# Sixteen slot-table scatters on GpSimd: taken out of the attention heads and issued in the first eleven slots of the shared experts

## The chip, the cores and the metric

One core of one Trainium2 chip runs the whole program. The metric is device time in microseconds (us), taken as the median of several runs. Lower is better.

## The reference: what is computed

One transformer layer on x (4 batches, 512 tokens, 512 features) and a context (4, 512, 256). First cross attention, then a mixture of experts:

```
x = x + xattn(layernorm(x), ctx)            # 16 heads of 32, softmax, keys 0..495 and 16 "dca" keys apart
h = layernorm(x)                            # 2048 tokens
scores = softmax(h @ gate_w.T)              # 64 experts
w6, e6 = top_k(scores, 6); w6 /= sum(w6)    # 12288 (token, expert) pairs
pos = place of the pair among its expert's pairs;  dropped if pos >= 384
y[token] += w6 * expert_e(h[token])         # silu(h@wg.T) * (h@wu.T) @ wd.T, 352 wide
out = x + y + shared_expert(h)              # 704 wide, every token
```

## The kernel before, in words

Everything is fp32. Products that need accuracy are split into a rounded high part and a rest (names ending in `_hi`, `_lo`). Each engine has its own written-out program, and semaphores tie them together.

**Heads.** The 2048 tokens are 16 tiles of 128; there are 64 heads (4 batches of 16). A loop over `UNITS`, u = 0 to 15, does four heads each (`n = 4 * u` and on) and threads through them the work of several tiles at different stages: the q, k and v products of later tiles, the output projection of tile u - 5 (`wo_product`), its second layer norm, and the routing of tile u - 6. On TensorE a head is: transposes of the negated maxima (`shift_turned`, L1400), score products (L1415), transposed score products (`turn_scores`, L1425), and the weighting of the values of the head before (`weigh`, L1441 and L1444). VectorE takes the maxima (`maxima`, L643 to L645) and divides (`weighted`, L654, L656), ScalarE takes the exponentials (`exps`, L1104). GpSimd adds the two attention results of each head (`join`, L451), adds a bias (`with_bo`, L479), scales q and k (`scaled`, L442) and adds the mask of a tile to a running count (`counted_on`, L488).

**Routing of one tile j.** TensorE computes its logits (`route_logits`, L1503), VectorE copies them out (`take_logits`, L731) and TensorE's next `shift_turned` into the same bank waits for that copy. VectorE finds the six experts, TensorE the positions (`route_pos`), and VectorE writes, for each of 128 tokens, six slot numbers into `slot` and six pairs of (token number, weight) into `rows`; then `slot_ready` rises. These two buffers hold all 16 tiles, each in a place of its own.

**The scatter.** GpSimd writes the pairs of tile j to `slot_table` in HBM with six indirect DMAs, one for each of the token's experts, 128 rows of 8 bytes each (`scatter(j)`, L462). Each adds 16 to `tab_in`. Tiles 0 to 9 (`GROUP1` is 10) are routed in the heads, tile j in unit j + 6; tiles 10 to 15 are routed together in the first slots of the shared experts.

**Shared experts.** 16 slots, eight token blocks of 256 by two halves of the shared expert. In a slot TensorE does three gate/up chunks (`gate_up`, L2390, 24 matmuls each), then the down product of the item before (`down`, L2408), with transposes of the next block between (`transpose_chunk`, L2373). ScalarE takes the silu of a chunk (L2221), VectorE multiplies (L2297), and so on. TensorE may be up to three chunks ahead of VectorE's product (`sets = 3`). At named points of a slot a callback, `side(slot, point)`, does the rest of the heads' work: the layer norm and routing of the last tiles. On GpSimd only the point "rows" is used, at the head of the slot, and GpSimd has nothing else to do until it copies ids for the first routed expert. SyncE waits at the start of slot 11 for `tab_in` to reach 16 * 6 * 16, then loads the whole table; VectorE reads it in slot 12. After the 16 slots come the 64 routed experts, whose rows are gathered and added back by indirect DMAs.

**GpSimd's order in a unit of the heads** is: `scatter(u - 7)`, `join(n - 1)`, a part of the weights (`wo_part`), `with_bo(u - 2)`, `join(n)`, `counted_on`, `scaled` twice, a bias, `join(n + 1)`, a bias, `join(n + 2)`. After the last unit it does `join(63)`, `with_bo` twice and `scatter(9)`.

Of the kernel before, what the change touches and what calls it, by code (L numbers as in the profile page):

```python
# [58 lines left out]
TILES = NB * T  # L59
# [5 lines left out]
GROUP1 = TILES - 6  # L65
# [42 lines left out]
def attention_phase(nc, ctx, K, ins, hbuf, x1d, table, kvd, qkd):  # L108
    with ExitStack() as here:
# [18 lines left out]
        carry, slot, rows, xc, h2T, bst, mv2, eps5 = K.carry, K.slot, K.rows, K.xc, K.h2T, K.bst, K.mv2, K.eps5  # L128
# [144 lines left out]
        def tile(j):  # L273
            return 0 <= j < TILES
# [4 lines left out]
        def keys_of(j):  # L279

            return P - DCA if j % T == T - 1 else P
# [153 lines left out]
        def heads_gpsimd(pool, net):  # L435
            def scaled(j, v, col, given, done):
                if not tile(j):
                    return
                pool.wait_ge(rs_ready.sem, rs_ready.value(j - 5, 0))
                g = heads_of(v[:, j % 2, :])  # L440
                scale = rs[:, (j - 5) % 2, col:col + H]
                pool.tensor_tensor(g, g, bc(scale.unsqueeze(2), [P, H, HD]), ALU.mult).then_inc(done.sem, 1)  # L442

            def join(n):
                if not head(n):
                    return
                b, h = n // H, n % H
                pool.wait_ge(pv_taken.sem, pv_taken.value(n, 1))
                if h == 0 and b >= 2:
                    pool.wait_ge(aoT_ready.sem, aoT_ready.value((b - 1) * T - 1, 1))  # L450
                pool.tensor_tensor(ao_of(b)[:, :, h * HD:(h + 1) * HD], pv2[:, n % 2, :, 0, :],  # L451
                                   pv2[:, n % 2, :, 1, :], ALU.add).then_inc(head_done.sem, 1)

            def scatter(j):
                if not tile(j):
                    return
                if j == 0:
                    pool.wait_ge(scratch_and_wo, SCRATCH_AND_WO)
                pool.wait_ge(slot_ready.sem, slot_ready.value(j, 1))
                pool.sem_inc(passed, 1)  # L460
                for k in range(TOPK):
                    pool.indirect_dma_start(  # L462
                        out=table, out_offset=bass.IndirectOffsetOnAxis(slot[:, j, k:k + 1], 0),
                        in_=rows[:, j, k, :], in_offset=None, bounds_check=E * CAP - 1,
                        oob_is_err=False).then_inc(tab_in, 16)

            def biased(j, m, v, bias, raw, done):
                if not tile(j):
                    return
                pool.wait_ge(raw.sem, raw.value(j, 1))  # L470
                pool.tensor_tensor(v[0:m, j % 2, :], v[0:m, j % 2, :], bias[0:m, :], ALU.add).then_inc(done.sem, 1)

            def with_bo(j):
                if not tile(j):
                    return
                if j == 0:
                    pool.wait_ge(scratch_and_wo, SCRATCH_AND_WO)
                pool.wait_ge(xc_in[j % 2].sem, xc_in[j % 2].value(j // 2, 16))
                pool.tensor_tensor(xc[:, j % 5, :], xc[:, j % 5, :], bo[:], ALU.add).then_inc(xb_ready.sem, 1)  # L479

            def counted_on(j):
                if not tile(j):
                    return
                pool.wait_ge(mask_ready.sem, mask_ready.value(j, 1))
                if j >= 1:
                    pool.wait_ge(carry_ready.sem, carry_ready.value(j - 1, 1))
                    pool.wait_ge(pos_ready.sem, pos_ready.value(j - 1, 1))
                pool.tensor_tensor(carry[:, (j + 1) % 2, :], carry[:, j % 2, :], mask[:], ALU.add).then_inc(carry_ready.sem, 1)  # L488
# [105 lines left out]
            def wo_part(c):  # L594
                if c == 0:
                    pool.wait_ge(scratch_and_wo, SCRATCH_AND_WO)
                    pool.wait_ge(kvd_ready, 1)
                if c >= DC:
                    return
                src = wo_in_place[:, c * D:(c + 1) * D]  # L600
                pool.tensor_copy(wo_hi[:, c, :], src)
                pool.drain()
                pool.tensor_tensor(wo_lo[:, c, :], src, wo_hi[:, c, :].bitcast(F32), ALU.subtract).then_inc(pool_split, 1)
# [3 lines left out]
                front(u + 7)  # L607
            for u in UNITS:
                n = 4 * u
                scatter(u - 7)  # L610
                join(n - 1)
                wo_part(u)

                with_bo(u - 2)
                join(n)

                counted_on(u - 6)
                scaled(u + 5, kb, H, k_sum, kn_ready)
                scaled(u + 5, qb, 0, q_sum, qn_ready)
                biased(u + 6, P, qb, bq, q_raw, q_bias)  # L620
                join(n + 1)

                biased(u + 6, keys_of(u + 6) if tile(u + 6) else P, kb, bk, k_raw, k_bias)
                join(n + 2)
            join(HEADS - 1)
            with_bo(TILES - 2)
            with_bo(TILES - 1)
            scatter(GROUP1 - 1)

            def side(slot, point):  # L630
                if point == "rows" and GROUP1 <= slot + 4 < TILES:
                    scatter(slot + 4)
            return side

# [752 lines left out]
        def heads_tensor(pe, net):  # L1387
# [396 lines left out]
            def side(slot_no, point):  # L1784
# [21 lines left out]
                elif here == (5, "chunk1"):  # L1806
# [3 lines left out]
            return side  # L1810

        return dict(sync=heads_sync, gpsimd=heads_gpsimd, vector=heads_vector, scalar=heads_scalar, tensor=heads_tensor,
                    over_made=over_made, h2_out=h2_out, x1_out=x1_out, wo_ready=wo_ready)

# [1012 lines left out]
```

## Time and profile before

| | |
|---|---|
| median of 3 runs | 1850.05 us (1841.58, 1850.05, 1877.37) |
| the profiled execution's own time | 1846.09 us |
| its span, first to last instruction | 1844.4 us |
| mean granted TensorE clock | 0.955 of full |
| busy: TensorE matmuls, VectorE, ScalarE, GpSimd | 1766.3, 1091.5, 1029.9, 742.0 us |
| heads | about 88 to 675 us of the span |
| shared experts' slots | about 690 to 897 us |

Times in the text are microseconds from the start of the span. A line such as L1503 is a line of the kernel file. PE is TensorE's matmul row and PEld its weight loads, DVE is VectorE, ACT is ScalarE, POOL is GpSimd, SP is SyncE. PEclk is the granted TensorE clock: 1.00 is 2.4 GHz, 0.50 is 1.2 GHz.

### The profile page before, as it was taken

Reading aid. Unit: us, or ns where it says so; the run is one execution under the profiler, and the core shown is the slowest. Engines: PE = TensorE matmul, PEld = TensorE weight load, DVE = VectorE, ACT = ScalarE, POOL = GpSimd, SP = SyncE. Lnnn points to the kernel's source line nnn. Section 1 sums busy time; section 2 is a strip of 40 time slices with the busy share of each in tenths; the row PEclk is TensorE's granted clock in tenths of the full one; section 3 lists DMA queues with packets and bytes.
Section 4 is the critical chain, followed back from the end, with each engine's and each line's share of the span. In section 5 each row is a group of like instructions: output and inputs, shape, how many; then the busy total and the mean of one; then the engine's idle time right before and its main releaser. Section 6 shows DMA issues by size and latency. Waiting matters only on the chain.

```text
span 1844.4 us, 36478 instructions
## 1 busy us (share of the span) xinstructions
PE 1766.3 (96%) x12110; PEld 1614.3 (88%) x12110; DVE 1091.5 (59%) x2166; ACT 1029.9 (56%) x1879; POOL 742.0 (40%) x711
## 2 busy tenths in 40 slices
PE   3799999999999999999999999999999999999997
PEld 3588888888888878999999999999999999999986
DVE  6555657666555644434466666666666666666655
ACT  4567666556534535112366666666666666666654
POOL 6522222333213220034035555555555545555532
PEclk8999999899769879999999999999999999999988
DMA  5533433332312512411268777777777777786765
GB/s 179 163 109 105 111 98 104 98 88 84 90 58 61 175 40 81 150 65 53 88 199 242 207 217 221 209 229 209 239 202 222 216 214 223 215 232 204 234 185 167
DMA packets 149083, 289.89 MB, mean 157 GB/s; under 512 B 29198, under 2 KB 66318, under 8 KB 139648
## 3 DMA queue, kind: packets, MB, share of 16 engines
q1 hardware_dynamic: 116112, 238.21, 39.6%
q0 software_dynamic: 32880, 50.51, 13.0%
q8 instruction: 52, 0.85, 0.2%
q14 instruction: 39, 0.32, 0.1%
HBM read 243.73 MB, written 64.52 MB: 167 GB/s over the span
## 4 chain that ended last, share of the span: by engine, by line
PE 85%; DVE 4%; issue 4%; ACT 2%; POOL 1%; DVEq 1%; another core or an unknown queue 1%; DMA 1%; SPq 0%; ACTq 0%; POOLq 0%
PE ps L2390 36%; PE ps L2408 18%; PE ps L1444 8%; PE ps L1452 5%; PE ps L1425 4%; PE ps L2373 3%; PE ps L1415 3%; PE ps L1441 2%; PE ps L1467 1%; PE ps L1400 1%; PE ps L2712 1%; PE ps L1461 1%; DVE nmax L643 1%; DVEq L645 0%
## 5 line engine op out<-in xcount | busy, mean ns | idle before, releaser
L2140 POOL DMA_INDIRECT out<-y,ids_s x128 | 204.8, 1600 | 283.5 <-ACT y L2271 258.7
L2390 PE MATMUL ps<-xt_hi,gu_hi 128*128 128x256 f32 (+1 forms) x1920 | 313.6, 285 | 0.0
L2390 PE MATMUL ps<-xt_lo,gu_hi 128*128 128x256 f32 (+1 forms) x1920 | 299.8, 278 | 0.0
L2390 PE MATMUL ps<-xt_hi,gu_lo 128*128 128x256 f32 (+1 forms) x1920 | 299.2, 278 | 0.0
L1104 ACT ACTIVATE prob<-ps 128x512 f32<-128x512 f32 x256 | 151.9, 597 | 238.2 <-PE ps L1425 193.9
L2175 DVE TENSOR_TENSOR gu_lo<-raw_gu,gu_hi 128x1408 fp32r<-128x1408 f32 x132 | 214.5, 1625 | 114.0 <-ACT gu_hi L2172 104.1
L2390 PEld LDWEIGHTS ps<-xt_hi,gu_hi 128*128 128x128 f32 (+1 forms) x1920 | 259.4, 180 | 6.9
L2390 PEld LDWEIGHTS ps<-xt_lo,gu_hi 128*128 128x128 f32 (+1 forms) x1920 | 252.1, 179 | 0.0
L2390 PEld LDWEIGHTS ps<-xt_hi,gu_lo 128*128 128x128 f32 (+1 forms) x1920 | 251.8, 179 | 0.0
L2120 POOL DMA_INDIRECT xg<-h_rows,ids_g x128 | 192.9, 1507 | 119.9 <-POOL ids_g L2115 50.6
L2228 ACT ACTIVATE h_hi<-h 128x256 fp32r<-128x256 f32 (+1 forms) x240 | 100.5, 419 | 227.2 <-DVE h L2297 226.7
L1444 PE MATMUL ps<-v_main,prob 128*128 128x33 f32 x1536 | 225.7, 287 | 0.0
L1444 PEld LDWEIGHTS ps<-v_main,prob 128*128 128x128 f32 x1536 | 212.2, 209 | 0.0
L643 DVE TENSOR_REDUCE nmax<-ps 128x2 fp32r<-128x992 f32 x128 | 152.3, 1189 | 74.7 <-PE ps L1415 68.8
L2221 ACT ACTIVATE sg<-ps 128x256 f32<-128x256 f32 (+1 forms) x240 | 90.9, 379 | 180.8 <-PE ps L2390 128.5
L2172 ACT ACTIVATE gu_hi<-raw_gu 128x1408 fp32r<-128x1408 f32 x132 | 180.8, 1370 | 0.0
L462 POOL DMA_INDIRECT slot_table<-rows,slot x96 | 97.0, 1011 | 163.1 <-DVEq L1061 135.1
L2297 DVE TENSOR_TENSOR h<-sg,ps 128x256 f32<-128x256 f32 (+1 forms) x240 | 99.4, 414 | 76.7 <-ACT sg L2221 63.8
L2408 PE MATMUL ps<-d_hi,h_hi 128*128 128x512 f32 (+1 forms) x480 | 138.1, 396 | 0.0
L2408 PE MATMUL ps<-d_lo,h_hi 128*128 128x512 f32 (+1 forms) x480 | 137.9, 395 | 0.0
L2408 PE MATMUL ps<-d_hi,h_lo 128*128 128x512 f32 (+1 forms) x480 | 137.9, 395 | 0.0
L1425 PE MATMUL ps<-qs,ks 128*128 128x512 f32 x256 | 131.8, 516 | 0.7 <-ACT qs L1096 0.7
(305 smaller groups left out, 3041.0 us busy)
## 6 DMA issues: line engine op xcount, KB each, us to landing
raw_gu<-in_w_gu SPq DMA_DIRECT2D x71, 1408.0 KB
raw_d<-in_w_d SPq DMA_DIRECT2D x71, 512.0 KB
raw_d<-in_w_d SPq DMA_DIRECT2D x71, 192.0 KB
qs<-qk_rows SPq DMA_DIRECT2D x192, 64.0 KB, 1.9
ks<-qk_rows SPq DMA_DIRECT2D x192, 64.0 KB, 2.0
xa<-in_x SPq DMA_DIRECT2D x16, 256.0 KB, 2.9
qk_rows<-k_hi SPq DMA_DIRECT2D x16, 256.0 KB, 2.2
qk_rows<-k_lo SPq DMA_DIRECT2D x16, 256.0 KB, 2.5
```

The source lines that it names most:

```text
L643: dve.tensor_reduce(nmax[:, n % 2, t, 0], ps[:, SCB:SCB + 2, 0:MAIN], AX, ALU.max, negate=True)
L1104: act.activation(prob[:, n % 2, c, :], ps[:, STB + c % 2, :], ACT.Exp).then_inc(prob_ready.sem, 1)
L1425: pe.matmul(ps[:, STB + c % 2, :], ks[:, n % RING, c * P:(c + 1) * P], qs[:, n % RING, :], start=True, stop=True).then_inc(sT_ready.sem, 1)
L1444: last = pe.matmul(ps[:, POB, o:o + HD + 1], prow[:, c, :], v_main[:, b % 2, c, h, :], start=False, stop=c == T - 2)
L2120: pool.indirect_dma_start(out=B.xg[:, p, k, :], out_offset=None, in_=hbuf, in_offset=bass.IndirectOffsetOnAxis(B.ids_g[:, p, k:k + 1], 0), ...
L2140: pool.indirect_dma_start(out=out, out_offset=bass.IndirectOffsetOnAxis(B.ids_s[:, p, k:k + 1], 0), in_=B.y[:, p, k, :], in_offset=None, b ...
L2172: eng.activation(hi, raw, ACT.Copy).then_inc(gu_hi.sem, 1)
L2175: eng.tensor_tensor(B.gu_lo[:, p, half], raw, hi.bitcast(F32), ALU.subtract).then_inc(gu_lo.sem, 1)
L2228: act.activation(B.h_hi[0:m, it.half, c, 0:W], B.h[0:m, (it.half * NF + c) % 2, 0:W], ACT.Copy).then_inc(h_hi.sem, 1)
L2297: dve.tensor_tensor(B.h[0:m, b, 0:W], B.sg[0:m, b, 0:W], gu_banks(c, m)[1], ALU.mult).then_inc(h_ready.sem, 1)
L2390: last = pe.matmul(gu_banks(c, m)[half], w[:, p, half, d, o:o + m], x[:, x_p, d, 0:W], start=i == 0, stop=i == len(steps) - 1)
L2408: last = pe.matmul(ps[:, Y0 + k % 2, :], h[0:m, p, c, k * P:(k + 1) * P], w[0:m, p, c, :], start=begins and i == 0, stop=ends and i == len ...
```

## The change

The scatters of tiles 0 to 9 leave the heads. In the callback, slots 0 to 4 issue two tiles each (0 and 1, 2 and 3, up to 8 and 9), and slots 6 to 11 issue tiles 10 to 15 as before. The number of indirect DMAs stays at 96; nothing else is touched.

```diff
             for u in UNITS:
                 n = 4 * u
-                scatter(u - 7)
                 join(n - 1)
                 wo_part(u)
...
             with_bo(TILES - 2)
             with_bo(TILES - 1)
-            scatter(GROUP1 - 1)

             def side(slot, point):
-                if point == "rows" and GROUP1 <= slot + 4 < TILES:
+                if point != "rows":
+                    return
+                if slot < GROUP1 // 2:
+                    scatter(2 * slot)
+                    scatter(2 * slot + 1)
+                if GROUP1 <= slot + 4 < TILES:
                     scatter(slot + 4)
             return side
```

## Rows read from the trace of the kernel before

**Rows 1.** The page: busy time, and the chain that ended last, by engine.

```profile
PE 1766.3 (96%) x12110; PEld 1614.3 (88%) x12110; DVE 1091.5 (59%) x2166; ACT 1029.9 (56%) x1879; POOL 742.0 (40%) x711
...
PE 85%; DVE 4%; issue 4%; ACT 2%; POOL 1%; DVEq 1%; another core or an unknown queue 1%; DMA 1%; SPq 0%; ACTq 0%; POOLq 0%
```

**Rows 2.** Stretches: length, busy time (instructions) of each engine, PEclk, DMA share, GB/s.

```profile
120.00:300.00 180.00, 178.81 (x1226) 158.38 (x1225) 106.10 (x217) 122.86 (x212) 45.10 (x55) 1.00 0.39 109
...
313.60:674.50 360.90, 345.06 (x2044) 302.64 (x2044) 209.67 (x545) 175.90 (x307) 101.30 (x124) 0.84 0.29 87
...
509.20:555.70 46.50, 45.03 (x210) 39.99 (x209) 22.23 (x60) 16.65 (x28) 9.21 (x12) 0.64 0.18 52
555.70:588.10 32.40, 31.31 (x210) 27.10 (x209) 20.52 (x56) 16.53 (x28) 9.21 (x12) 0.94 0.26 75
```

**Rows 3.** GpSimd's groups (busy, mean ns, idle before) and waits: the scatter.

```profile
L462 POOL DMA_INDIRECT slot_table<-rows,slot x96 | 97.0, 1011 | 163.1 <-DVEq L1061 135.1 <-issue 28.0
...
POOL slot_table L462 <- DVEq L1061: 135.1, 6, 108.1
```

**Rows 4.** Timeline of unit 6, without a scatter: start, length, instruction, [idle before, releaser].

```profile
284.16 1.00 PE L1503 MATMUL ps<-wg,h2T 128*128 128x64 f32 x8
...
285.87 0.48 PE L1425 MATMUL ps<-qs,ks 128*128 128x512 f32 x1
...
285.29 0.22 DVE L731 COPY lg<-ps 128x64 f32<-128x64 f32 x1
...
286.38 0.60 ACT L1104 ACTIVATE prob<-ps 128x512 f32<-128x512 f32 x1 [1.82 <-PE ps L1425]
```

**Rows 5.** Timeline of unit 14 at the same place, beside the end of scatter(7).

```profile
595.01 1.00 PE L1503 MATMUL ps<-wg,h2T 128*128 128x64 f32 x8
...
596.72 0.48 PE L1425 MATMUL ps<-qs,ks 128*128 128x512 f32 x1
...
599.33 0.60 PE L1400 MATMUL ps<-ident,nmax 128*32 128x128 f32 x4 [1.02 <-DVE lg L731]
...
598.96 0.23 DVE L731 COPY lg<-ps 128x64 f32<-128x64 f32 x1 [2.46 <-remote]
...
599.06 1.09 ACT L1104 ACTIVATE prob<-ps 128x512 f32<-128x512 f32 x2 [3.71 <-PE ps L1425]
...
596.72 0.97 POOL L462 DMA_INDIRECT slot_table<-rows,slot  x1 [0.30 <-issue]
```

**Rows 6.** Sum over nine stretches, each from a scatter's end, about 3 us long.

```profile
sum 26.17, PE 18.64 PEld 15.24 DVE 15.58 ACT 12.89 POOL 5.23; mean PE 2.07 PEld 1.69 DVE 1.73 ACT 1.43 POOL 0.58
```

**Rows 7.** Stretches at the lower clock that begin beside a scatter's end.

```profile
327.40:334.20 6.80, 6.80 (x24) 5.66 (x24) 4.62 (x12) 2.01 (x5) 0.00 (x0) 0.50 0.49 147
364.90:375.10 10.20, 9.31 (x34) 7.74 (x35) 7.18 (x15) 4.47 (x10) 1.74 (x3) 0.50 0.42 117
...
521.90:559.50 37.60, 37.60 (x149) 33.63 (x148) 17.40 (x49) 13.78 (x23) 4.64 (x8) 0.50 0.21 61
```

**Rows 8.** Slots 7 and 8 of the shared experts, beside scatter(10) and scatter(11).

```profile
800.57 0.62 PE L2390 MATMUL ps<-xt_hi,gu_lo 128*128 128x256 f32 x4
...
803.62 0.39 ACT L2221 ACTIVATE sg<-ps 128x256 f32<-128x256 f32 x1 [8.05 <-remote]
...
794.00:807.00 13.00, 13.00 (x97) 12.21 (x96) 5.11 (x12) 2.84 (x8) 5.83 (x6) 1.00 0.34 119
...
813.50 0.62 PE L2390 MATMUL ps<-xt_hi,gu_lo 128*128 128x256 f32 x4
...
814.16 0.38 ACT L2221 ACTIVATE sg<-ps 128x256 f32<-128x256 f32 x1 [4.75 <-PE ps L2390]
```

**Rows 9.** Timeline of the passage from heads to slots: PE, DVE, POOL.

```profile
707.79 1.54 PE L1767 MATMUL ps<-wg,h2T 128*128 128x64 f32 x6 [4.15 <-ACT h2T L1235]
...
683.22 1.62 DVE L2175 TENSOR_TENSOR gu_lo<-raw_gu,gu_hi 128x1408 fp32r<-128x1408 f32 x1
...
683.47 2.21 POOL L462 DMA_INDIRECT slot_table<-rows,slot  x1 [0.30 <-issue]
```

## The prediction

> **What bounds the kernel now.** The page first: TensorE's matmuls are busy 96% of the span and hold 85% of the chain that ended last; GpSimd has 1% of it [rows 1]. So a change on GpSimd counts only through what it does to TensorE: its idle time, and the clock it is granted. I therefore cut the span into stretches. From 120 to 300 us, heads without any scatter, TensorE idles 1.19 of 180 us and the clock is 1.00. From 313.6 to 674.5 us, the units that hold the nine scatters of tiles 0 to 8, it idles 360.9 - 345.06 = 15.8 us and the mean clock is 0.84, so the half clock (1.2 GHz) ran for 2 x 0.16 x 360.9 = 115 us [rows 2]. That is the stage to read.
>
> **What a scatter is on its own engine.** 96 instructions of 1.011 us, with 0.3 us of issue between (28.0 us over 90) [rows 3]: six take 7.7 us. In the heads `join(n - 1)` is behind them, but after a scatter GpSimd still waits for VectorE before that join (2.46 us in unit 14, whose scatter ends at 597.7), so its own time costs nothing there. By this count alone the change gives zero.
>
> **What a scatter does to TensorE's signals.** Look at one place of a unit, with and without a scatter. In unit 6 the logits (L1503) end at 285.16 and VectorE copies them at 285.29; the score product L1425 ends at 286.35 and ScalarE starts at 286.38 [rows 4]. In unit 14 the same two end at 596.01 and 597.20, but the copy starts at 598.96 and the exponential at 599.06: 2.9 and 1.9 us late, both idle, neither with a cause that the profile can name ("remote" for one). Both start 1.3 us after the scatter's last DMA ends at 597.69. TensorE then waits 1.02 us, because `shift_turned` needs the copy [rows 5]. I read it so: late in a burst of six small scatters, the semaphore updates of TensorE reach the others late. The same holds in slot 7: a chunk ends at 801.19, ScalarE starts at 803.62, "remote", 1.3 us after scatter(10); but there TensorE is up to three chunks ahead, and its stretch has 13.00 busy of 13.00 [rows 8]. This is inferred: no row shows an update in transit.
>
> **The change, part by part.**
> Removed from the heads, idle time: the nine stretches right after the scatters hold 26.17 - 18.64 = 7.5 us of TensorE idle [rows 6]. Bounds: 0 (another late wait takes each place) and 7.5. I take 7.5 here, and price what comes in its place apart, below.
> Removed from the heads, half clock: three of its stretches, 6.8, 10.2 and 37.6 us long, begin within 3 us of a scatter's end (324.8, 365.0 and 518.8) [rows 7]; 54.6 us together. The price of one: unit 12 and unit 13 run the same 210 matmuls in 46.5 and 32.4 us with clocks of 0.64 and 0.94 [rows 2], that is 33.5 and 3.9 us at half clock, so 14.1 / 29.6 = 0.48 us for each us of it. 54.6 x 0.48 = 26 us. Bounds: 0 (the drops come at other gaps instead) and all 115 us, 55 us (without its gaps the stretch looks like that before 300, at 1.00). I take 26: what followed the scatters goes, the rest stays. As a check, the scatters' share of the idle time (7.5 of 15.8) and of the half clock (54.6 of 115) are both 47%.
> In its place: with the copy on time, the next late thing in these units is VectorE's own routing work and maxima. The idle time that is not beside a scatter is 8.3 us over nine units; I let half as much again appear, 4 us, with no clock on top. Bounds 0 and 8.
> Added in the slots: GpSimd is free from about 677.5 us, and slots 0 to 4 have no other wait on it, so tiles 0 to 9 go out in one train, not two per slot of TensorE: 60 x 1.28 = 77 us, to about 755. `scatter(10)` waited 108.1 us for VectorE and starts at 795 [rows 3], so the train ends 40 us before it, and the table load in slot 11 doesn't move. The longest instruction of the trace is 2.21 us, beside a wide subtraction on VectorE [rows 9]; if all 60 were such, the train would take 60 x 2.5 = 151 us and push scatter(10) by 33 us. I don't expect that: the mean is 1.01.
> What is queued behind the train on GpSimd: only scatter(10). Its 96 DMAs still all count into `tab_in`, for which SyncE waits long after.
> Who pays for the train: TensorE's signals in slots 0 to 4. In steady slots nothing, by the 13.00 of 13.00. The passage is tight: TensorE idles 4.15 us at 707.79 for the transposed rows [rows 9], after output product, residual, norm and transposes, each handed over by a signal. Two of its signals are on that path; held by 0 to 2.9 us each, I take 1.5 for both, 3 us, and 1 us for the positions in slot 4: 4 us. Bounds 0 and 12 (four holds of 2.9).
>
> **The sum**, against the profiled execution's own 1846.1 us: 1846.1 - 7.5 - 26 + 4 + 4 = 1820.6. I say **1821 us**. The profiled execution is 4 us below the median of 1850.05, and the three runs lie 36 us apart, which is 2%: half-clock stretches that come and go could make that. A difference under 2% is about what a measurement of this kernel can't tell from none.
>
> **Rules weighed.** Row: VectorE's subtraction keeps its 1.62 us while the indirect DMA beside it takes 2.21 instead of 0.97 [rows 9]. The Trainium skill (SBUF — State Buffer, Who interferes with whom) has the two engines lock each other out of a shared port, whoever is first; by that rule the train is stretched beside wide VectorE work, and the trace agrees in this one row.
> Row: ScalarE and VectorE start 1.9 to 2.9 us late beside a scatter [rows 5]. The same section of the Trainium skill says that only that port pair causes contention, that TensorE and ScalarE wait on no one, and that DMA takes nothing from a compute engine. By this rule the late starts have another cause, and the change would be worth nothing.
>
> **The rivals.**
> (a) *Nothing comes of it*: the late starts belong to the place in the unit, not to the scatter. They would then stay: 1846. For it: the scatter always stands at the same place, and the rule above. Against it: unit 6 and slot 7.
> (b) *Only the gaps go*: the clock falls at other gaps. 1846.1 - 7.5 + 4 = 1843. For it: other stretches at half clock don't begin at a scatter (60 of the 115 us), and a gap of 1.02 us in unit 14 cost no clock.
> (c) *The whole clock returns*: the heads run as before 300 us: 1846.1 - 7.5 - 55 + 4 = 1788. For it: 180 us at 1.00 without a scatter. Against it: units 7 to 15 have VectorE's routing work too.
> (d) *Slower*: the last hold ends only when the burst does; if a train of 60 holds signals to its end, TensorE runs its three chunks ahead (3 x 2.7 = 8 us from 690) and stands until about 756, some 57 us, less the 33.5 gained, and a restart at half clock: 1870, and up to 1905 if the port stretches the train. It decides once one hold lasts longer than those 8 us. Against it: at 813.50 + 0.62 a chunk ends inside the burst of scatter(11), 5.8 us after its start, and ScalarE begins at 814.16, at once [rows 8]; so signals get through in a burst.
>
> **Chances.** Forecast (1808 to 1835) 0.48, (a) 0.12, (b) 0.20, (c) 0.13, (d) 0.07. The range 1798 to 1852 takes in the forecast, (a) and (b), and the near part of (c). Faster by over 2% means below 1813: (c) and a third of the forecast's case, 0.29. Slower by over 2% means above 1887: half of (d), 0.03. The rest, 0.68, is within 2%.
>
> **What would show it.** In the profile of the changed kernel: 60 scatters back to back from about 677.5 to 755 us; no start marked "remote" on ScalarE or VectorE in the heads, and the copy L731 within 0.3 us of the logits; PE idle from 313 to the end of the heads about 8 to 12 us instead of 15.8; PEclk there about 0.92 instead of 0.84; more idle at the first logits L1767 than 4.15 us; scatter(10) still released by VectorE. The prediction is wrong if the late starts remain without scatters (a), if PEclk stays near 0.84 though the gaps went (b), or if TensorE idles by tens of us in slots 0 to 4 (d).

## The result, and the profile after

The changed kernel takes 1854.57 us (median of 22 runs, 1844.04 to 1871.39), the kernel before, measured beside it, 1843.61 us (22 runs, 1824.2 to 1877.37). The ratio is 1.0082, 95% interval 1.0054 to 1.011: slower by 0.8%, where 1821 us were forecast. The profiled execution of the changed kernel has a span of 1868.7 us and a time of its own of 1870.5 us, among the slowest of its 22, so its losses are at the large end. Lines of the kernel behind the edit are three higher: L1503 is L1506, L731 is L734, L2390 is L2393.

The page first: busy time, the chain by engine, then three groups of the gate/up product.

```profile
PE 1748.7 (94%) x12110; PEld 1595.6 (85%) x12110; DVE 1090.7 (58%) x2166; ACT 1030.1 (55%) x1879; POOL 740.8 (40%) x711
...
PE 83%; issue 5%; DVE 5%; ACT 2%; another core or an unknown queue 1%; DVEq 1%; POOL 1%; DMA 1%; SPq 0%; ACTq 0%; POOLq 0%
...
L2393 PE MATMUL ps<-xt_hi,gu_hi 128*128 128x256 f32 (+1 forms) x1920 | 316.8, 286 | 15.9 <-issue 15.6
L2393 PE MATMUL ps<-xt_lo,gu_hi 128*128 128x256 f32 (+1 forms) x1920 | 302.9, 279 | 20.3 <-issue 20.3
L2393 PE MATMUL ps<-xt_hi,gu_lo 128*128 128x256 f32 (+1 forms) x1920 | 302.5, 279 | 16.3 <-issue 16.3
```

TensorE is busy 17.6 us less than in [rows 1], in a span 24.3 us longer, so it stands more (the mean granted clock over the span is 0.955 in both). The last three rows say where it stands: 52 us before gate/up matmuls, and not for a semaphore but for "issue", a wait for nothing that the profile shows. Next the stretches, columns as in [rows 2], of the changed kernel and then of the kernel before. They are cut at `join(63)`, which ends the heads, and at scatter(10).

```profile
300.00:633.60 333.60, 323.33 (x2140) 284.61 (x2138) 217.46 (x566) 185.89 (x326) 53.13 (x74) 0.94 0.32 98
633.60:656.00 22.40, 19.79 (x96) 16.09 (x96) 13.32 (x22) 8.19 (x11) 18.13 (x17) 0.85 0.15 49
656.00:720.00 64.00, 12.50 (x34) 8.68 (x34) 7.22 (x15) 6.45 (x13) 45.61 (x46) 0.52 0.05 13
720.00:815.00 95.00, 94.07 (x705) 88.61 (x706) 38.21 (x113) 29.24 (x66) 0.00 (x0) 0.96 0.31 110
```

```profile
300.00:674.50 374.50, 357.84 (x2139) 314.19 (x2137) 218.20 (x565) 185.95 (x325) 106.64 (x129) 0.85 0.29 88
674.50:795.00 120.50, 114.26 (x836) 107.05 (x837) 58.45 (x150) 43.45 (x90) 10.77 (x9) 0.97 0.29 102
```

The heads did what was hoped, and more. They end at 633.6 instead of 674.5 us, 40.9 us earlier: the idle time falls from 16.7 to 10.3 us, and the half clock from 2 x 0.15 x 374.5 = 112 to 2 x 0.06 x 333.6 = 40 us (72 x 0.48 = 35 us). From there to scatter(10) the changed kernel needs 181.6 us instead of 120.5, 61.1 us more. Of these, 48.8 are idle time (55.0 against 6.2); for the other 12 there is the clock, 0.52 from 656 to 720 us where it was 0.97 over the whole passage. Behind scatter(10) 4.1 us more are lost. -40.9 + 61.1 + 4.1 = +24.3, the difference of the two spans.

The place of [rows 5] in the changed kernel, unit 14, now without a scatter beside it:

```profile
590.55 1.00 PE L1506 MATMUL ps<-wg,h2T 128*128 128x64 f32 x8
...
592.22 0.23 DVE L734 COPY lg<-ps 128x64 f32<-128x64 f32 x1 [0.19 <-issue]
592.25 0.48 PE L1428 MATMUL ps<-qs,ks 128*128 128x512 f32 x1
...
592.77 0.60 ACT L1107 ACTIVATE prob<-ps 128x512 f32<-128x512 f32 x1 [1.89 <-PE ps L1428]
```

The exponential starts 0.04 us behind its product, where it was 1.9 us late. The copy starts 0.67 us behind the logits, and not for a signal but because VectorE was still at work: its idle time before it is 0.19 us of issue. Now the beginning and the body of the train, as TensorE, ScalarE, VectorE and GpSimd see it (timeline, the same kernel):

```profile
654.74 0.38 PE L2376 MATMUL ps<-ident,xg 128*128 128x128 f32 x2 [0.28 <-issue]
655.45 0.27 PE L2376 MATMUL ps<-ident,xg 128*128 128x128 f32 x1 [0.34 <-issue]
656.85 0.52 PE L2393 MATMUL ps<-xt_hi,gu_hi 128*128 128x256 f32 x3 [1.13 <-issue]
...
694.29 0.37 PE L2393 MATMUL ps<-xt_hi,gu_hi 128*96 128x256 f32 x1 [2.43 <-issue]
697.11 0.37 PE L2393 MATMUL ps<-xt_hi,gu_hi 128*96 128x256 f32 x1 [2.45 <-issue]
699.91 0.37 PE L2393 MATMUL ps<-xt_hi,gu_hi 128*96 128x256 f32 x1 [2.43 <-issue]
...
701.33 0.38 ACT L2224 ACTIVATE sg<-ps 128x256 f32<-128x256 f32 x1 [39.52 <-issue]
706.24 0.38 ACT L2206 ACTIVATE xt_hi<-ps 128x256 fp32r<-128x256 f32 x1 [4.53 <-remote]
711.84 0.38 ACT L2206 ACTIVATE xt_hi<-ps 128x256 fp32r<-128x256 f32 x1 [5.21 <-remote]
...
722.47 0.38 ACT L2224 ACTIVATE sg<-ps 128x256 f32<-128x256 f32 x1 [7.27 <-remote]
...
701.75 0.42 DVE L2300 TENSOR_TENSOR h<-sg,ps 128x256 f32<-128x256 f32 x1 [39.79 <-issue]
...
636.71 1.19 POOL L462 DMA_INDIRECT slot_table<-rows,slot  x1 [0.16 <-issue]
```

GpSimd's train begins at 636.7. TensorE signals twice for these transposes, once for each 128 of the features: the first signal belongs to the transposes that end at 655.0, the second to those that end at 655.72. ScalarE takes them at 706.24 and 711.84, 51 and 56 us later. TensorE itself crawls: its matmuls come mostly singly, 0.7 to 2.8 us apart and steadily 2.8 from 689 on, and nothing in the kernel makes it wait. ScalarE and VectorE stand for almost 40 us each. The train is over at 715.5; at about 721 TensorE is back at its pace, and at 722.47 the train's last late start comes. The signals that arrive inside the train (701, 706 and 712) are 47 to 56 us late, and one waits past its end. So it isn't only that the others learn late of TensorE's work: TensorE's own instructions come late.

The prediction said that no row shows an update in transit. The traces keep records of semaphore updates, with their times, and these go further. In the kernel before, unit 14, the update for the logits is recorded at 598.94, 2.9 us behind their end and 0.02 us ahead of the copy; here the two updates for the transposes stand at 706.22 and 711.82. So the waiting engines start as soon as the count rises, and what is late is the update. What the other engines tell one another in the same train is not: ScalarE's product of 701.33 ends at 701.71, and VectorE starts on it at 701.75. Since the ends of matmuls are modelled, the trace can't say whether a product itself was late or only its signal.

The Trainium skill (SBUF — State Buffer, Who interferes with whom) says that TensorE and ScalarE wait on no one and that a DMA takes nothing from a compute engine. These rows don't agree with it as a rule for what a DMA can cost a kernel: 51.5 of 64 us stand beside indirect DMAs. No row shows that SBUF's ports are where it happens.

### The profile page after: what moved, and what is told of

Read it like the earlier page. It is cut to its first block, busy times and chain, and to the rows that moved or that the text cites. A ratio compares the mean times of both kernels' runs of the same rounds, so it can differ in the third digit from the quotient of the medians.

```text
span 1868.7 us, 36478 instructions
## 1 busy us (share of the span) xinstructions
PE 1748.7 (94%) x12110; PEld 1595.6 (85%) x12110; DVE 1090.7 (58%) x2166; ACT 1030.1 (55%) x1879; POOL 740.8 (40%) x711
## 4 chain that ended last, share of the span: by engine, by line
PE 83%; issue 5%; DVE 5%; ACT 2%; another core or an unknown queue 1%; DVEq 1%; POOL 1%; DMA 1%; SPq 0%; ACTq 0%; POOLq 0%
PE ps L2393 35%; PE ps L2411 18%; PE ps L1447 7%; PE ps L1455 5%; PE ps L1428 3%; PE ps L2376 3%; PE ps L1418 3%; PE ps L1444 2%; PE ps L2715 1%; PE ps L1470 1%; PE ps L1403 1%; DVE nmax L646 1%; DVEq L648 1%; PE ps L1464 1%
## 5 line engine op out<-in xcount | busy, mean ns | idle before, releaser
L2393 PE MATMUL ps<-xt_hi,gu_hi 128*128 128x256 f32 (+1 forms) x1920 | 316.8, 286 | 15.9 <-issue 15.6
L2393 PE MATMUL ps<-xt_lo,gu_hi 128*128 128x256 f32 (+1 forms) x1920 | 302.9, 279 | 20.3 <-issue 20.3
L2393 PE MATMUL ps<-xt_hi,gu_lo 128*128 128x256 f32 (+1 forms) x1920 | 302.5, 279 | 16.3 <-issue 16.3
L2393 PEld LDWEIGHTS ps<-xt_hi,gu_hi 128*128 128x128 f32 (+1 forms) x1920 | 260.6, 180 | 24.4 <-issue 17.5
L2393 PEld LDWEIGHTS ps<-xt_lo,gu_hi 128*128 128x128 f32 (+1 forms) x1920 | 254.1, 180 | 20.8 <-issue 20.8
L2393 PEld LDWEIGHTS ps<-xt_hi,gu_lo 128*128 128x128 f32 (+1 forms) x1920 | 253.7, 180 | 19.5 <-issue 19.5
L1447 PE MATMUL ps<-v_main,prob 128*128 128x33 f32 x1536 | 212.7, 277 | 0.0
L1447 PEld LDWEIGHTS ps<-v_main,prob 128*128 128x128 f32 x1536 | 198.7, 198 | 0.0
L646 DVE TENSOR_REDUCE nmax<-ps 128x2 fp32r<-128x992 f32 x128 | 152.1, 1189 | 61.1 <-PE ps L1418 57.7
L2305 DVE TENSOR_TENSOR h_lo<-h,h_hi 128x256 fp32r<-128x256 f32 (+1 forms) x240 | 100.4, 418 | 46.0 <-ACT h_hi L2231 45.1
```

The costliest lines, as they stand in the source:

```text
L646: dve.tensor_reduce(nmax[:, n % 2, t, 0], ps[:, SCB:SCB + 2, 0:MAIN], AX, ALU.max, negate=True)
L1447: last = pe.matmul(ps[:, POB, o:o + HD + 1], prow[:, c, :], v_main[:, b % 2, c, h, :], start=False, stop=c == T - 2)
L2305: dve.tensor_tensor(B.h_lo[0:m, it.half, c, 0:W], B.h[0:m, (it.half * NF + c) % 2, 0:W], B.h_hi[0:m, it.half, c, 0:W].bitcast(F32), ALU.su ...
L2393: last = pe.matmul(gu_banks(c, m)[half], w[:, p, half, d, o:o + m], x[:, x_p, d, 0:W], start=i == 0, stop=i == len(steps) - 1)
```

## The experiments

Eighteen runs in nine sessions; the runs of a session share a chip and runs of the kernel before. "Before" below is the kernel before in the same session.

**First session: spacing the DMAs, and moving the train.**

e1_singles, the kernel before with the six DMAs of a tile apart:

```diff
-                scatter(u - 7)
+                j = u - 7
+                scatter(j, [0])
                 join(n - 1)
                 wo_part(u)
-
+                scatter(j, [1])
                 with_bo(u - 2)
...
                 join(n + 2)
+                scatter(j, [5])
```

> The kernel before, but the six indirect DMAs of a tile no longer stand in a row: one stands at each of six places of the unit, with a join, a bias or a scaling between. Theory A (TensorE's semaphore updates are held up only once several of these DMAs have been issued without a pause, and the longer the chain the worse): no start marked remote on ScalarE or VectorE in the heads, the heads end near 634 us as in the changed kernel, the passage and slots stay as before (join 63 to scatter(10) 120 us), so 41 us come off: about 1805 us. Theory B (every such DMA holds the updates for about a microsecond, however they are spaced): six short holds a unit instead of one long one, heads end near 675 us, about 1845 us. Theory C (the gain of the heads came from the engine time of GpSimd, not from signals): GpSimd's joins come 1 us later each, so the heads end near 675 us too.

e2_landed and e3_train_landed, the same two lines in the kernel before and in the changed one:

```diff
                 for k in range(TOPK):
+                    if j * TOPK + k > 0:
+                        pool.wait_ge(tab_in, 16 * (j * TOPK + k))
                     pool.indirect_dma_start(
```

> The kernel before, but each indirect DMA waits until the one before it has landed (tab_in at 16 times their number), in the same places. Theory A1 (what holds the updates is a backlog of DMAs issued faster than they are carried out): no backlog, no late start, heads end near 634 to 645 us although each scatter takes longer on GpSimd. Theory A2 (what holds them is GpSimd's issuing itself, not the backlog): the pauses of about 2 us between DMAs let updates through, so holds shrink to under 1 us each; the two differ in the lateness left beside a DMA. Theory B: the holds stay and spread over a longer burst, heads end at 675 us or later.

> The changed kernel, but each indirect DMA waits until the one before it has landed. Theory A (A1 or A2): the train of 60 lasts about 60 times 3 us = 180 us instead of 77, and pushes scatter(10) to about 815 us, yet TensorE keeps its pace in the passage and first slots (idle 5 to 15 us from 634 to 720 us instead of some 66), and the time is 1800 to 1825 us. Theory B (each of the 60 holds TensorE's signals or issue by a fixed price): the loss of about 61 us against the slots of before stays, about 1865 us.

e4_late_train, the changed kernel with the train behind slot 1 (`K.line` holds the semaphores of the shared experts' slots, here that of VectorE's products):

```diff
-                if slot < GROUP1 // 2:
-                    scatter(2 * slot)
-                    scatter(2 * slot + 1)
+                if slot == 2:
+                    pool.wait_ge(K.line.h_ready.sem, K.line.h_ready.value(1, NF))
+                    for j in range(GROUP1):
+                        scatter(j)
```

> The changed kernel, but the train of 60 starts only when VectorE has finished the products of slot 1, past the passage, where TensorE ran without a gap in both kernels. Theory A: the slots have no protection either: TensorE's three chunks ahead are used up in 8 us and its own issue crawls, so TensorE idles 50 to 65 us beside the train and the time stays near 1865 us. Theory P (the passage is what is tight; in steady slots a train costs nothing, as the stretch 794 to 807 us of the kernel before suggested): TensorE idles under 5 us beside the train, heads gain 41 us, about 1805 us, at most 15 more for the later scatter(10).

| | us | before us | |
|---|---|---|---|
| e1_singles | 1811.56 | 1805.89 | ratio 1.0022 (0.9985 to 1.006) |
| e2_landed | 1910.73 | 1805.89 | one run |
| e3_train_landed | 1910.98 | 1805.89 | one run |
| e4_late_train | 1810.68 | 1805.89 | one run |

None of them can be read as it was meant, for one reason: the kernel before took 1806 us here, not 1844 (13 runs, 1798.52 to 1816.87), so there was nothing left to gain. And the late train of 60 cost nothing. A stretch of e4_late_train with nearly the whole train in it:

```profile
690.00:790.00 100.00, 100.00 (x748) 93.90 (x747) 41.79 (x121) 22.19 (x58) 73.44 (x76) 1.00 0.28 92
```

GpSimd is busy 73 us with 76 instructions, and TensorE has no gap at all. That could be the place (theory P) or the session; the second session decides it. e2 and e3 show something else, the price of a wait for landing. e3_train_landed, one scatter DMA, then the longest waits from 790 to 940 us:

```profile
635.90 0.97 POOL L464 DMA_INDIRECT slot_table<-rows,slot  x1 [1.91 <-DMA slot_table<-rows,slot]
```

```profile
DVE ids L2292 <- DMA slots<-slot_table: 118.7, 1, 118.7
...
PE ps L2395 <- DVE h L2302: 104.4, 1, 104.4
```

One DMA now takes at least 0.97 + 1.91 = 2.88 us instead of 1.28. All 96 together get the table out so late that VectorE, whose products stand behind the read of the table, holds TensorE for 104.4 us. In e2 the same wait stretches a scatter in the heads from 7.7 to 16 us; the joins behind it come late, and TensorE idles 401.2 - 370.58 = 30.6 us from 300 us to the end of the heads at 701.2, with a clock of 0.82. The Trainium skill (Perfetto Trace Analysis, DMA Instruction — SWDGE) says that the end of such an instruction is the end of GpSimd's part, not of the transfer; the 1.91 us behind it agree.

**Second session: both kernels again, unchanged** (c1_before, c2_after).

> The kernel before, unchanged, for a second profile: on the chip of the first experiments it took 1806 us where it had taken 1844 us, and no kernel there shows a late signal of TensorE. Theory A (the hold depends on the chip, or on where the program lies in it, and not on the kernel): on a chip where it takes about 1806 us its trace has no start marked remote beside a scatter and the heads end near 634 us; on a chip where it takes about 1845 us they are there again and the heads end near 675 us. Theory B (the hold belongs to the kernel, and the first experiments removed it by their edits): late starts in any case, and the 1806 us come from elsewhere.

> The changed kernel, unchanged, beside the kernel before on this same chip. Theory A: where the kernel before takes about 1806 us there is no hold to lose or to gain, and the two are within 5 us of one another; where it takes about 1845 us, the changed one takes 1855 us, with the crawl of TensorE beside the train of 60. Theory B (the train itself costs, on any chip): the train costs some 20 to 60 us here too, since the DMAs are the same.

c1_before takes 1807.91 us (one run), c2_after 1806.44 us beside 1806.25: ratio 1.0000, interval 0.9973 to 1.0026. Theory B of both falls. Timeline of c1_before, unit 14, inside the same burst of scatter(7) as in [rows 5]:

```profile
595.61 0.97 POOL L462 DMA_INDIRECT slot_table<-rows,slot  x1 [0.30 <-issue]
...
596.05 0.48 PE L1425 MATMUL ps<-qs,ks 128*128 128x512 f32 x1
...
596.57 0.60 ACT L1104 ACTIVATE prob<-ps 128x512 f32<-128x512 f32 x1 [4.10 <-PE ps L1425]
...
597.18 0.48 PE L1425 MATMUL ps<-qs,ks 128*128 128x512 f32 x1
...
597.69 0.60 ACT L1104 ACTIVATE prob<-ps 128x512 f32<-128x512 f32 x1 [0.53 <-PE ps L1425]
...
598.15 0.97 POOL L462 DMA_INDIRECT slot_table<-rows,slot  x1 [0.30 <-issue]
```

Six DMAs at the same pace of 1.27 us, from 591.8 to 599.1, and ScalarE starts 0.04 and 0.03 us behind TensorE in their midst. Stretches of c1_before and then of c2_after, in which the train of 60 begins at 632.5:

```profile
300.00:631.00 331.00, 320.07 (x2174) 282.13 (x2172) 222.84 (x583) 190.71 (x334) 108.79 (x133) 0.97 0.34 100
631.00:690.00 59.00, 53.74 (x356) 49.54 (x356) 29.45 (x59) 30.36 (x55) 8.24 (x8) 0.89 0.23 80
```

```profile
300.00:631.00 331.00, 320.47 (x2162) 282.25 (x2160) 220.98 (x572) 188.58 (x331) 54.74 (x76) 0.96 0.33 100
631.00:690.00 59.00, 53.27 (x375) 50.00 (x376) 30.28 (x61) 30.88 (x57) 46.50 (x43) 0.94 0.25 81
690.00:790.00 100.00, 100.00 (x742) 93.70 (x741) 44.10 (x125) 21.16 (x58) 37.64 (x39) 1.00 0.31 108
```

The same instructions, and neither the gain nor the loss. So there are two conditions. With **holds**, TensorE's signals come late beside these DMAs, and the kernel before takes about 1844 us. In the **free** one none is late, and it takes about 1806 us: in none of its sixteen traces does an idle ScalarE start over 0.3 us behind its score product, its chunk or its transposes. All kernels of a session met the same one.

Two more things in the traces bear on what holds are. The DMAs themselves run alike: the last packet of each DMA's rows ends a median of 0.75 us behind its instruction in the train with holds (at most 1.09) and 0.76 us in that of c2_after, so no backlog of transfers stands behind the holds. And with holds, records of updates are missing. The profile gives no time to landing for the down weights of the routed experts in any of the four traces with holds (the two first profiles, f1_double and f2_sixes below), and gives one in all sixteen free ones; here the kernel before, then c1_before:

```profile
raw_d<-in_w_d SPq DMA_DIRECT2D x71, 512.0 KB
...
raw_d<-in_w_d SPq DMA_DIRECT2D x71, 512.0 KB, 3.9
```

Of the 1536 updates of `tab_in`, all of which must have come for SyncE to go on, the traces keep 591 (before), 421 (after) and 549 (f2_sixes) with holds, and all 1536 in c1_before. So late signals and lost records of updates go together. That raises a rival which no run here tests: that the recording itself takes part in the holds, and that a kernel which is not recorded meets none. Every time on record comes with a recorded span and clock, so none here speaks against it.

**Third session: longer and shorter rows** (another chip; it met holds, before 1840.03 us). f1_double issues each DMA of the changed kernel a second time, into a table that nobody reads, and waits for 2 x 96 of them. f2_sixes cuts the train (`gu_ready` is TensorE's count of finished chunks):

```diff
-                if slot < GROUP1 // 2:
-                    scatter(2 * slot)
-                    scatter(2 * slot + 1)
+                if slot < GROUP1:
+                    if slot > 0:
+                        pool.wait_ge(K.line.gu_ready.sem, K.line.gu_ready.value(slot - 1, NF))
+                    scatter(slot)
```

> The changed kernel with every indirect DMA of the scatters issued twice, the second time into a table of its own that nobody reads: a train of 120 instead of 60, about 154 us long, and 12 DMAs in a slot from slot 7 on. Theory A (holding is a state of the chip): where the kernel before takes 1806 us, nothing is held here either, TensorE has no gap beside the train, and what is left is that scatter(10) starts later, about 790 instead of 754 us, and the table perhaps with it: 1806 to 1825 us. Where the kernel before takes about 1845 us, the crawl lasts as long as the train: some 70 to 80 us on top of 1855. Theory B (there is one limit on all chips, and the train of 60 stays just under it on the first): 120 DMAs pass it, and starts of ScalarE and VectorE come late and gaps stand on TensorE on any chip.

> The changed kernel, but the train is cut into bursts of six: one tile in each of slots 0 to 9, released when TensorE has finished the slot before (with tiles 10 to 15 in slots 6 to 11 as they were). Theory A: where the kernel before takes 1806 us, 1806 again; where it takes about 1845 us, the heads keep their gain of 41 us and holds of at most 3 us stay hidden in slots whose TensorE has three chunks in hand: about 1805 us. Theory B (the sum of DMAs counts, not the length of a burst): where the train costs 60 us in one piece, it costs them in ten.

f1_double takes 1960.73 us, f2_sixes 1835.94 us (one run each). Stretches of f1_double, with the train of 120 in them:

```profile
620.00:690.00 70.00, 42.36 (x258) 37.42 (x258) 21.67 (x40) 20.27 (x37) 54.63 (x51) 0.76 0.18 58
690.00:790.00 100.00, 16.87 (x38) 9.95 (x39) 3.01 (x5) 3.02 (x6) 67.43 (x69) 0.50 0.03 6
```

TensorE gets 38 matmuls done in 100 us, beside some 750 in e4. The time is 26 us above the 1935 expected of theory A: beside the rows of twelve that follow, from 860 to 990 us, TensorE idles another 23 us. Stretches of f2_sixes, slots with six DMAs each and then slots with twelve each (tile s and tile s + 4 in one slot):

```profile
690.00:755.00 65.00, 65.00 (x495) 61.13 (x495) 28.55 (x93) 13.55 (x39) 23.91 (x25) 1.00 0.34 117
755.00:815.00 60.00, 46.01 (x276) 39.74 (x275) 14.08 (x31) 8.16 (x23) 35.06 (x36) 0.84 0.15 46
```

Rows of six: no gap in 65 us. Rows of twelve: 14 of 60 us. The first of them, timeline of f2_sixes:

```profile
754.93 0.97 POOL L462 DMA_INDIRECT slot_table<-rows,slot  x1 [6.10 <-DVEq L1065]
...
759.78 0.62 PE L2394 MATMUL ps<-xt_hi,gu_lo 128*128 128x256 f32 x4
...
762.50 0.62 PE L2394 MATMUL ps<-xt_hi,gu_lo 128*128 128x256 f32 x4
...
764.97 0.40 PE L2394 MATMUL ps<-xt_lo,gu_hi 128*96 128x256 f32 x2 [0.69 <-issue]
766.42 0.28 PE L2394 MATMUL ps<-xt_hi,gu_lo 128*96 128x256 f32 x1 [1.06 <-issue]
...
763.57 0.38 ACT L2225 ACTIVATE sg<-ps 128x256 f32<-128x256 f32 x1 [8.20 <-PE ps L2394]
...
772.22 0.38 ACT L2225 ACTIVATE sg<-ps 128x256 f32<-128x256 f32 x1 [7.36 <-remote]
```

A chunk ends at 760.40, 5.5 us into the row, and its signal arrives at 763.57: 3.2 us late, but inside the row. At about 764.3 TensorE starts to falter; the chunk that ends at 763.12 is heard of at 772.22, 9.1 us late and after the last DMA has ended at 770.0. Beside rows of six the signals are late too, by up to 2.6 us, but that stays hidden behind the chunks in hand. Theory B falls: the same 96 DMAs cost less in short rows than in one train. Theory A, the length of the unbroken row, fits. Not told apart from it is the number of DMAs in some 20 us, since the rows of twelve also stand closer together: 36 DMAs in 60 us, where it was 24 in 65. The heads of f2_sixes end at 633.7 as in the changed kernel. From there to the first gather of the routed experts it takes 223 us where the kernel before took 198 (674.5 to 872.0): the 14 us beside the rows of twelve are the largest part that I can place.

**Fourth to eighth session: rows of four, reads, and the search for the condition.** g1_chunks spreads all 96 DMAs over slots 0 to 11, at most four in a row:

```diff
+                todo = [(j, k) for j in range(GROUP1) for k in range(TOPK)]
+                if slot < 6:
+                    part = todo[10 * slot:10 * slot + 10]
...
+                third = (len(part) + 2) // 3
+                for c in range(3):
+                    if slot + c > 0 and part:
+                        before = slot * NF + c - 1
+                        pool.wait_ge(K.line.gu_ready.sem, K.line.gu_ready.value(before // NF, before % NF + 1))
+                    for j, k in part[c * third:c * third + third]:
+                        scatter(j, [k])
```

g2_singles is e1_singles. g3_reads is the kernel before with 60 reading DMAs more:

```diff
+                if slot < GROUP1 // 2:
+                    pool.sem_inc(passed, 1)
+                    for j in range(2 * slot, 2 * slot + 2):
+                        for k in range(TOPK):
+                            pool.indirect_dma_start(
+                                out=K.probe[:, j, k, :], out_offset=None, in_=pairs,
+                                in_offset=bass.IndirectOffsetOnAxis(places[:, j, k:k + 1], 0),
+                                bounds_check=E * CAP - 1, oob_is_err=False).then_inc(tab_in, 16)
```

> The changed kernel, but in the slots no more than four indirect DMAs stand in a row: ten a slot in slots 0 to 5 and six in slots 6 to 11, each third of them released when TensorE has finished another gate/up chunk. In f2_sixes TensorE stood still only beside the rows of twelve (14 us from 755 to 815 us), not beside those of six. Theory A (length of the unbroken row, on a chip that holds at all): where the kernel before takes about 1840 us, no gap beside a scatter in heads or slots, heads end near 634 us and 198 us later the first gather: about 1800 us. Where it takes 1806 us, no difference: 1800 to 1810 us. Theory B (the number of DMAs in the slots counts): about 14 us lost in the slots, as in f2_sixes, or more.

> The same kernel as e1_singles (the kernel before with a tile's six indirect DMAs each in a place of its own among the joins of the heads), on this chip. On the first chip it gave 1.0022 of the kernel before. Theory A: where the kernel before takes about 1840 us, no start is late in the heads, they end 25 to 40 us earlier than 675 us, about 1805 to 1815 us; where it takes 1806 us, 1.00 again. Theory B (every DMA has its own price for TensorE's signals): about 1840 us beside 1840.

> The kernel before, with its scatters where they were, and a train of 60 indirect DMAs more in slots 0 to 4 that read 8 byte rows of x into a buffer of their own (nobody uses them) where the changed kernel writes 8 byte rows. Theory W (the writes of 8 bytes to HBM are what clogs): reads leave TensorE alone, no crawl in the passage, within 5 us of the kernel before on this chip. Theory I (the issuing of indirect DMAs, 128 rows each, without pause is what clogs): the same crawl as in the changed kernel where the chip holds, some 60 us slower than the kernel before; nothing where it doesn't.

The fourth session ran on the chip of the third and met the free condition: the kernel before took 1803.06 us, where one run of it had taken 1840.03 half an hour earlier. So it isn't the chip alone. The repeats, on two more chips at least, were meant to meet holds:

> The kernel of g1_chunks again (at most four indirect DMAs in a row, all in slots 0 to 11), since the call of g1_chunks met the condition without late signals. If the kernel before takes about 1840 us here: theory A (length of the unbroken row) 1800 to 1810 us and no TensorE gap beside a scatter; theory B (their number) a loss in the slots as in f2_sixes, 1830 us or more. If it takes about 1806 us: 1.003 of it again.

> The kernel of g3_reads again (the kernel before and a train of 60 reading indirect DMAs in slots 0 to 4). If the kernel before takes about 1840 us here: theory W (the 8 byte writes clog) 1840 us, no crawl; theory I (the issuing clogs) about 1900 us, with TensorE crawling beside the train. If it takes about 1806 us: no difference again, as in g3_reads (1805 beside 1803 us).

> The kernel of g1_chunks again. If the kernel before takes about 1840 us here: theory A (length of the unbroken row) 1800 to 1810 us and no TensorE gap beside a scatter; theory B (their number) 1830 us or more, with gaps in the slots as in f2_sixes. If it takes about 1806 us: 1.00 of it again.

> The kernel of g1_chunks again. If the kernel before takes about 1840 us here: theory A (length of the unbroken row) 1800 to 1810 us and no TensorE gap beside a scatter; theory B (their number) 1830 us or more, with gaps in the slots as in f2_sixes. If it takes about 1806 us: 1.00 of it again.

> The kernel of g3_reads again. If the kernel before takes about 1840 us here: theory W (the 8 byte writes clog) 1840 us, no crawl; theory I (the issuing clogs) about 1900 us, with TensorE crawling beside the train. If it takes about 1806 us: no difference again.

> The kernel of g1_chunks again. If the kernel before takes about 1840 us here: theory A (length of the unbroken row) 1800 to 1810 us and no TensorE gap beside a scatter; theory B (their number) 1830 us or more, with gaps in the slots as in f2_sixes. If it takes about 1806 us: 1.00 of it again.

| | us | before us | |
|---|---|---|---|
| g1_chunks | 1806.31 | 1803.06 | ratio 1.003 (1.0004 to 1.0055) |
| h1_chunks | 1807.03 | 1805.43 | ratio 1.0003 (0.998 to 1.0026) |
| i1_chunks | 1808.30 | 1805.83 | ratio 1.001 (0.9976 to 1.0045) |
| j1, k1_chunks | 1805.77, 1806.48 | 1806.05, 1798.50 | one run each |
| g2_singles | 1819.20 | 1803.06 | ratio 1.0076 (1.0046 to 1.0105) |
| g3, h2, j2_reads | 1805.20, 1809.13, 1797.10 | 1803.06, 1805.43, 1806.05 | one run each |

None met them. In the free condition rows of four cost nothing that matters, reads cost nothing, and single DMAs among the joins cost 0.8% in one session and nothing measurable in the other. That chunks or reads behave so with holds was not shown.

**The last: f1_double again** (l1_double), whose row of 120 had met only holds.

> The kernel of f1_double again (the changed kernel, every scatter DMA issued twice, a train of 120). If the kernel before takes about 1806 us here: theory N (no hold at all in this condition) no crawl of TensorE beside the train; the only cost is that the last scatters, 12 DMAs a slot, end later and the table with them, at most some 20 us: 1806 to 1830 us. Theory M (the threshold is only higher) a crawl in the second half of the train, 1850 us or more. If the kernel before takes about 1840 us: about 1960 us again.

It takes 1866.61 us beside 1799.51. Its stretches, and its longest waits from 790 to 895 us:

```profile
690.00:790.00 100.00, 100.00 (x741) 93.70 (x741) 44.45 (x125) 20.94 (x58) 74.30 (x76) 1.00 0.33 108
790.00:850.00 60.00, 40.81 (x291) 37.72 (x289) 10.74 (x24) 6.72 (x19) 45.68 (x48) 0.88 0.02 2
```

```profile
DVE ids L2294 <- DMA slots<-slot_table: 74.7, 1, 74.7
...
PE ps L2397 <- DVE h L2304: 60.3, 1, 60.3
```

Theory N: beside 120 DMAs without pause TensorE is busy 100.00 of 100.00, where f1_double had 16.87. The free condition isn't a higher threshold, at least up to a row of 120. The time is above the 1830 expected of theory N and in the range of theory M, but for another reason: the last scatters end at 887, the table comes late, and TensorE stands 60.3 us behind VectorE's read of it. I had taken 20 us for that.

## Why the prediction was wrong

The forecast was made from a profile in the condition with holds, and both measurements of the result (1854.57 and 1843.61 us) show it too. There its steps came out so:

- **That the late starts belong to the scatter**: right. Matched one by one with their score products, 10 of the 256 exponentials of the heads start over 0.3 us late in the kernel before (the latest by 3.0 us), and none in the changed kernel; rival (a), 1846 us because nothing changes, is out, as is (b), since the clock came with the gaps. The free condition adds what the profile of before couldn't show: the DMAs alone don't do it.
- **-7.5 us of idle time, with 4 us of waits in its place**: 16.7 to 10.3 us, 6.4 gained. The gaps went; hardly anything took their place.
- **-26 us of half clock**: mis-sized, right in kind. 72 us of half clock went, not 54.6, worth 35 us; rival (c), all 115 us, is too much, since 40 are left. (One of the three stretches that the prediction lists begins 3.1 us behind its scatter's end and one 0.1 us ahead of it, not within 3 us behind; no sum hangs on it.)
- **A train of 77 us, scatter(10) not pushed**: right. It ran from 636.7 to 715.5.
- **+4 us for signals in the slots, bounds 0 and 12**: this is the step that failed. It measured 61 us. The step counted late signals, 0 to 2.9 us each, as beside six DMAs; the length of a hold is no constant of a burst, but grows with the row, to 56 us in this one. And TensorE, which waits for none of these DMAs, got its own matmuls off one at a time, up to 2.8 us apart. No term had that.
- **Rival (d)**, 1870 us with 57 us lost, is what happened, at 1870.5 us in the profiled execution and 61 us; it was given 0.07. Only its account of TensorE was incomplete: not three chunks ahead and then standing, but crawling. It was put aside for one row, the signal at 814.16 that came through 5.8 us into a burst [rows 8]. f2_sixes shows why that row could not carry it: there a signal gets through 8.6 us into a row, itself 3.2 us late, and the next one is held to the row's end. A burst of six lasts 7.7 us, so no row of the kernel before could show what the sixtieth DMA does. That its 1870 us meets the profiled execution to the microsecond is luck: the median is 16 us lower. The bound should have been the length of the train.

With the two sides at -41 and +61 us in the profiled execution, the median lies 3 us above 1852, the end of the range. In the free condition, nothing is there to gain or lose, and the ratio is 1.0000.

Open is what the conditions are, and whether the recording has a part in them. Shown is that one chip met both within half an hour, that every profile in a session shows the same, and that eight of nine sessions met the free one. Open too is whether reading DMAs hold signals, and whether rows of four would keep the 41 us of the heads. Of the versions measured with holds, f2_sixes (1836 beside 1840, one run each) alone came out below before, by less than one run can tell: the 22 runs of the kernel before spread over 53 us.

## What to carry to other kernels

Work on an idle engine is not free by its own time: look at what its DMAs do to the signals of the engine that bounds the kernel, and when you gather bursts into one row, bound the price by the length of the new row, not by what the old short ones cost. Keep such rows short (six in a row cost no gap in slots with chunks in hand, twelve cost 14 of 60 us), but not by waiting for each landing, which makes each 2.88 us instead of 1.28. Before you explain a difference of 2%, time the kernel before in another session: here it moved by 38 us between sessions while nothing in it had changed.

## What the runs showed of the hardware

- In one condition a row of indirect DMAs from GpSimd, each 128 rows of 8 bytes, 1.27 us apart, lets TensorE's semaphore updates through for some 5 to 9 us and then delays them, most of them to the end of a short row or a microsecond or two past it: by up to 3.0 us beside six, over 9 beside twelve, and 56 beside sixty. Updates between ScalarE and VectorE in the train of sixty are on time.
- In the same rows TensorE's own matmuls come mostly singly, up to 2.8 us apart (34 in 64 us beside sixty, 38 in 100 beside 120), with "issue" as the only cause in the profile.
- The packets of these DMAs end as soon behind their instructions as in the other condition (0.75 and 0.76 us), and a part of the update records is missing from the trace (421 to 591 of 1536 kept for `tab_in`).
- In the other condition the same instructions, even 120 in a row, leave TensorE at 100.00 busy of 100.00 us.
- A wait for the landing of such a DMA ends 1.91 us after the end of its instruction, at the least.
